# Six of eight query, key, value and gate preparations from scaled fp16 halves in three products, with the instruction order laid out anew

## The reference

```python
x = x + 0.5 * ffn(layernorm(x), W_gate, W_qkv)
x = x + attn(layernorm(x), gamma, beta, W_in, ...)
x = x + 0.5 * ffn(layernorm(x), W_gate, W_qkv)

def ffn(x, W_gate, W_qkv):                       # 16 heads of 16
    gating = softmax(x @ W_gate.T)               # one expert of 16 for each row
    indicator = one_hot(argmax(gating))
    q, k, v = split(x @ W_qkv.T, 3)
    k_shared = sum_h indicator[h] * k[h]         # one key and one value head for all queries
    v_shared = sum_h indicator[h] * top1 * v[h]
    att = softmax(causal(q_h @ k_shared.T / 4))
    return att @ v_shared
def attn(x, ...):                                # h = (1-a) h + a b, y = h * tanh(c)
    gates = layernorm2(x) @ W_in + b_in
    return scan(gates) @ W_out + x @ W_skip + biases
```

## Time and profile before

| | |
|---|---|
| median of three runs | 1006.3 us (1001.84 to 1007.03) |
| the profiled execution | 999.46 us |
| its span, first to last instruction | 997.6 us |
| PE busy | 920.5 us (92%) |
| DVE busy | 789.8 us (79%) |
| ACT busy | 702.9 us (70%) |
| POOL busy | 195.4 us (20%) |
| mean granted TensorE clock | 0.946 of full speed |

### The profile page before, as it was taken

The page is one execution under the profiler, slowest core; times in us unless marked ns, Lnnn a source line. Parts: engine busy times, 40 slices in busy tenths (PEclk is TensorE's granted clock), DMA queues, the critical chain, the costliest instruction groups (busy, mean ns, idle before and its releaser), DMA issues.

```text
span 997.6 us, 17809 instructions
## 1 busy us (share of the span) xinstructions
PE 920.5 (92%) x6071; PEld 308.5 (31%) x6071; DVE 789.8 (79%) x2257; ACT 702.9 (70%) x1136; POOL 195.4 (20%) x408
## 2 busy tenths in 40 slices
PE   8988798989899998999998999999999999999997
PEld 6433242223232332222332234332233222222222
DVE  4899689999869898896136999799897999899501
ACT  2255447867557858789868756767767887788896
POOL 2023302110222010012312312422101100101115
PEclk7799599979989999999999999999999998999999
DMA  5110010000100010000001000100001000000001
GB/s 158 54 54 2 1 48 8 1 2 2 54 1 1 2 54 2 1 1 2 1 19 36 1 1 12 44 1 23 1 10 46 1 2 22 2 1 2 3 1 43
DMA packets 20232, 17.94 MB, mean 18 GB/s; under 512 B 4128, under 2 KB 20144, under 8 KB 20144
## 3 DMA queue, kind: packets, MB, share of 16 engines
q1 hardware_dynamic: 19328, 16.00, 5.2%
q10 hardware_dynamic: 816, 0.80, 0.2%
HBM read 10.24 MB, written 6.29 MB: 17 GB/s over the span
## 4 chain that ended last, share of the span: by engine, by line
PE 47%; DVE 34%; ACT 8%; issue 7%; POOL 2%; DMA 1%; SPq 0%; POOLq 0%; DVEq 0%; ACTq 0%
PE ps L1514 16%; DVE ps L1253 15%; DVE mxp L1250 10%; PE ps L1480 9%; PE ps L1502 8%; ACT probs L1082 6%; PE ps L1413 4%; DVE mxp L1253 3%; PE ps L1418 2%; PE ps L1446 2%; DVE kv L1221 2%; PE ps L1408 1%; PE ps L1453 1%; ACT relu L1070 1%; DVE prod L1212 1%
## 5 line engine op out<-in xcount | busy, mean ns | idle before, releaser
L1082 ACT ACTIVATE probs<-ps 128x1024 f32<-128x1024 f32 (+5 forms) x794 | 550.1, 768 | 147.0 <-PE ps L1502 143.8
L1250 DVE TENSOR_REDUCE mxp<-ps 128x1 f32<-128x512 f32 x512 | 319.4, 682 | 31.2 <-PE ps L1480 29.9
L1514 PE MATMUL ps<-probs,v_l 128*32 128x512 f32 (+3 forms) x2560 | 309.1, 563 | 13.2 <-POOL probs L882 10.2
L1480 PE MATMUL ps<-k_tl,q_t 48*128 48x512 f16 (+3 forms) x1152 | 250.8, 360 | 12.5 <-DVE mxp L1253 5.9
L1502 PE MATMUL ps<-q_t,k_tl 50*128 50x512 f16 (+3 forms) x1280 | 231.3, 361 | 26.2 <-DVE mxp L1253 6.1
L1253 DVE CUSTOM_DVE_ANT_0 ps<-ps,mask 128x384 f32<-128x384 f32 (+3 forms) x512 | 232.9, 526 | 23.7 <-PE ps L1480 22.7
L882 POOL TENSOR_SCALAR_AFFINE_SELECT probs<-probs 128x256 f32<-128x256 f32 x256 | 103.0, 412 | 577.8 <-ACT probs L1082 574.7
L1480 PEld LDWEIGHTS ps<-k_tl,q_t 48*128 48x128 f16 x1152 | 72.7, 96 | 198.8 <-DVE mxp L1250 67.2
L1502 PEld LDWEIGHTS ps<-q_t,k_tl 50*128 50x128 f16 x1280 | 62.0, 94 | 208.5 <-ACT probs L1082 86.6
L1253 DVE DVE_READ_ACCUMULATOR2_ANT mxp<- 128x1 f32 x640 | 89.6, 140 | 0.0
L1514 PEld LDWEIGHTS ps<-probs,v_l 128*32 128x32 f32 x2560 | 54.7, 110 | 109.4 <-issue 79.8
(11 more groups left out here) (129 smaller groups left out, 555.4 us busy)
## 6 DMA issues: line engine op xcount, KB each, us to landing
q_t<-q_scratch SPq DMA_DIRECT2D x96, 64.0 KB, 2.1
q_scratch<-q_part SPq DMA_DIRECT2D x16, 256.0 KB, 2.1
x_sb<-in_L_attn_x_dram SPq DMA_DIRECT2D x4, 512.0 KB, 8.1
out_dram<-x_sb SPq DMA_DIRECT2D x4, 512.0 KB, 2.9
q_t<-m_row SPq DMA_DIRECT2D x64, 4.0 KB
wqkv_n<-in_L_ffn_W_qkv_dram ACTq DMA_DIRECT2D x1, 768.0 KB, 6.5
w_in_sb<-in_L_attn_W_in_dram SPq DMA_DIRECT2D x1, 384.0 KB, 5.7
w_skip_sb<-in_L_attn_W_skip_dram SPq DMA_DIRECT2D x1, 256.0 KB, 5.0
```

The costliest lines, as they stand in the source:

```text
L1082: last = a_.activation(out if len(banks) == 1 else out[:, n:n + 1, :], bank[:, :, P * i:QW], ACT.Exp, scale=SCALE / LIFT ** 2)
L1250: last = v_.tensor_reduce(to, scores, axis=AX, op=ALU.max)
L1480: last = mm(bank[:, col:col + w], q_rows(ROWS_X, c, g, hh, i * P, P), keys, start=True, stop=True)
L1514: last = mm(out_bank[VW * hh:VW * hh + VW, P * i:QW], v_l[:, l, kt, :], probs[:, s % NB, hh, P * i:QW], start=j == 0, stop=j == key_tiles( ...
```

## The change

All preparations but (0, 0) and (0, 1) take another way, which `fine(l, c)` names. The deviation is scaled so that `u` comes out 1024 times larger. A new entry `halve` on POOL writes `u` as an fp16 number and the fp16 rest, `u_x`. `turn` transposes both parts with an fp16 identity, and ACT copies twice as many fp16 columns out of the bank into `ut_x`. The weights are scaled by a power taken from their largest square and also split in two fp16 parts, `wqkv_x` and `wg_x`, once: entries `size`, `scale` (two) and `split` (three), on DVE, PE, POOL and ACT. A float32 matmul becomes three fp16 matmuls (large by large, large by small, small by large). The scales are taken out again where the results are read (`z_inv`, `z_w`).

The planner gets the new entries and other estimates (a masked maximum 115 instead of 75, q 2100 instead of 1800 where float32, the start of its clock windows), and `SIDE_WORK` other places. Attention, maxima and recurrence are computed as before.

```diff
-SIDE_WORK = [(-19, -4, prepare(0, 1)), (18, 18, [("bias",)]), (18, 25, prepare(0, 2)), (57, 57, prepare(0, 3)),
-             (57, 69, branch(0)), (81, 81, prepare(1, 0)), (118, 140, branch(1)), (141, 141, prepare(1, 1)),
-             (154, 174, branch(2)), (174, 175, prepare(1, 2)), (175, 196, branch(3)), (210, 216, prepare(1, 3))]
+SPLIT = [("scale", n) for n in range(2)] + [("split", n) for n in range(3)]
+SIDE_WORK = [(-31, -4, prepare(0, 1)), (-4, 6, [("size",)] + SPLIT), (18, 18, [("bias",)]),
+             (24, 24, prepare(0, 2)), (60, 60, prepare(0, 3)), (64, 64, branch(0)), (80, 84, prepare(1, 0)),
+             (118, 140, branch(1)), (140, 140, prepare(1, 1)), (147, 174, branch(2)), (174, 175, prepare(1, 2)),
+             (175, 196, branch(3)), (210, 215, prepare(1, 3))]
...
-        self.stretch, self.streamed, self.full = 0.0, 0.0, True
+        self.stretch, self.streamed, self.full = FIRST_W - 1.0, 0.0, True
...
+            def halve(e):
+
+                pool.wait_ge(s_ln, NO["norm", e[1], e[2]] + 1)
+                own(g_.tensor_copy(u_x[:, 0, :, :], u[:, :, :]))
+                g_.tensor_tensor(u_x[:, 1, :, :], u[:, :, :], u_x[:, 0, :, :], op=ALU.subtract).then_inc(s_half, 1)
...
+                g_.tensor_tensor(z_root[:, :], z_sq[:, :], z_exp[:, :], op=ALU.pow).then_inc(s_zroot, 1)
...
+                elif e[0] == "turn" and fine(e[1], e[2]):
+                    a_.activation(ut_x[:, e[3], :, :].rearrange("p a t -> p (a t)"), bank[:, :].bitcast(f16), ACT.Copy)\
+                        .then_inc(s_ra, 1)
...
+                a_.activation(to, of, ACT.Copy, scale=z_mul[:, 0:1]).then_inc(s_wh, 1)
...
+                for dc in range(DC):
+                    v_.tensor_tensor(squared[:, dc * 3 * D:dc * 3 * D + 3 * D], wqkv_t[:, dc, :], wqkv_t[:, dc, :], op=ALU.mult)
+                own(v_.tensor_tensor(squared[:, 6 * D:6 * D + DC * H].rearrange("p (a h) -> p a h", a=DC), wg_t[:, :, :],
+                                     wg_t[:, :, :], op=ALU.mult))
+                v_.tensor_reduce(z_part[:, 0:1], squared[:, 0:6 * D + DC * H], axis=AX, op=ALU.max).then_inc(s_size, 1)
...
+                    v_.tensor_copy(z_sq[:, :], bank[:, 0:1]).then_inc(s_rd, 1)
+                    dve.wait_ge(s_zroot, 1)
+                    own(v_.tensor_scalar(z_mul[:, :], z_root[:, :], W_SIZE, None, ALU.mult))
+                    own(v_.reciprocal(z_inv[:, :], z_mul[:, :]))
...
+                v_.scalar_tensor_tensor(to, of, z_mul[:, 0:1], first, ALU.mult, ALU.subtract).then_inc(s_wx, 1)
...
+                    for a in range(2):
+                        for t in range(TC):
+                            last = tr(parts[:, a * QW + t * P:a * QW + (t + 1) * P], u_x[:, a, t, dc * P:(dc + 1) * P],
+                                      ident_h[:, :])
...
+                products = [(0, 0), (0, 1), (1, 0)]
...
+                elif kind == "kv" and fine(l, c):
+                    t = e[3]
+                    for n, (dc, (a, b)) in enumerate((dc, ab) for dc in range(DC) for ab in products):
+                        last = mm(bank[:, :], ut_x[:, dc, a, t * P:(t + 1) * P], wqkv_x[:, b, dc, D:3 * D],
+                                  start=n == 0, stop=n == 3 * DC - 1)
```

More of the change, by code:

```diff
@@ L117, in prepare @@
 def prepare(l, c):
-    return [("stats", l, c), ("norm", l, c), ("turn", l, c, 0), ("turn", l, c, 1), ("gate", l, c), ("pick", l, c),
+    return [("stats", l, c), ("norm", l, c)] + ([] if (l, c) in SINGLE else [("halve", l, c)]) + [("turn", l, c, 0), ("turn", l, c, 1), ("gate", l, c), ("pick", l, c),
             ("q", l, c, 0), ("kv", l, c, 0), ("choose", l, c, 0), ("qout", l, c, 0), ("q", l, c, 1),
@@ L161 @@
     "oev": (0, [("ACT", 480)]), "fin": (460, [("DVE", 700), ("POOL", 750)]), "out": (0, []),
+    "size": (0, [("DVE", 3600)]), "halve": (0, [("POOL", 3600)]),
     "join": (0, [("DVE", 750)]), "row": (100, [("ACT", 230)]),
 }
+HALVED = {"turn": (560, [("ACT", 920)]), "gate": (1500, WEIGHT["gate"][1]), "kv": (1350, WEIGHT["kv"][1]),
+          "q": (1350, WEIGHT["q"][1])}
 TO_READER, TO_PE, TO_NEXT = 205, 240, 130
@@ L187, in weights @@
         return 1.75 * width(e[1]), "columns", []
+    if e[0] == "scale":
+        return 100, "full", [("DVE", 2300 if e[1] else 700)]
+    if e[0] == "split":
+        return 0, "full", [("ACT", 750), ("DVE", 900)]
+    if e[0] in HALVED and len(e) > 2 and e[1] < 2 and e[1:3] not in SINGLE:
+        return HALVED[e[0]][0], "full", HALVED[e[0]][1]
     if e[0] == "range":
@@ L191, in weights @@
         kind, _, pieces = BANKS[UNITS[e[1]][1]][e[2]]
-        return 226, "rows", [("ACT", 480) if kind == "diff" else ("DVE", 600 if kind == "part" else sum(75 + 1.04 * w for *_, w, _ in pieces))]
+        return 226, "rows", [("ACT", 480) if kind == "diff" else ("DVE", 600 if kind == "part" else sum(115 + 1.04 * w for *_, w, _ in pieces))]
     if e[0] == "warm":
@@ L205, in needs @@
     k = e[0]
-    if k in ("norm", "turn", "gate", "pick", "q", "qout", "kv", "choose", "kpack", "keys"):
+    if k in ("norm", "halve", "turn", "gate", "pick", "q", "qout", "kv", "choose", "kpack", "keys"):
         l, c = e[1:3]
-        return {"norm": [("stats", l, c)], "turn": [("norm", l, c)], "pick": [("gate", l, c)],
+        fine = l < 2 and (l, c) not in SINGLE
+        return {"norm": [("stats", l, c)], "halve": [("norm", l, c)], "turn": [("halve" if fine else "norm", l, c)], "pick": [("gate", l, c)],
                 "qout": [("q",) + e[1:]], "choose": [("kv",) + e[1:], ("pick", l, c)],
-                "kpack": [("choose", l, c, TC - 1)], "keys": [("kpack", l, c)]}.get(k, [("turn", l, c, 1)])
+                "kpack": [("choose", l, c, TC - 1)], "keys": [("kpack", l, c)]}.get(k, [("turn", l, c, 1)] + ([("split", 2)] if fine else []))
     if k in ("dpack", "dkeys"):
@@ L218, in needs @@
         return [("rec", e[1], 1), ("skip", e[1], 1)]
+    if k in ("scale", "split"):
+        return [("scale", 1)] if k == "split" else [("scale", 0)] if e[1] else [("size",)]
     return [("squares",) if e[1] == 0 else ("range", 0)] if k == "range" else []
@@ L548, with fine @@
         _last = _e
+HALVES = [_e for _e in ORDER if _e[0] == "halve"]
+def fine(l, c):
+    return l < 2 and (l, c) not in SINGLE
 TURNS = [_e for _e in ORDER if _e[0] == "turn" and _e[3] == DC - 1]
@@ L1317, in _ @@
                     stats_of(e)
+                elif e[0] == "size":
+                    size()
+                elif e[0] == "scale":
+                    scales(e)
+                elif e[0] == "split":
+                    split(e)
                 elif e[0] == "squares":
```

116 lines of the change are left out of this document (104 added, 12 removed).

## The result

The changed kernel took 969.24 us (median of four, 966.6 to 972.44), the kernel before 1004.07 us beside it (four, 997.36 to 1007.03): ratio 0.966, 95% interval 0.9615 to 0.9706. The profiled execution, 972.44 us, is the slowest of the four. Single runs of the kernel before lie between 997 and 1010 us in all sessions, so a ratio of medians of a few runs is good to about 5 us.

What follows compares the result with a forecast made beforehand. PE and DVE were taken to share the bound, with PE setting the pace in the six changed preparations. -15.8 + 6 + 1 + 1 - 3 - 2 = -12.8 us off 1006.3 gave 993.5 us, range 983 to 1007.

Steps and rivals of the forecast that it cites:

- The order: Masks ahead of the statistics behind the bias entry, -3 us (bounds 0 and -5); warm matmuls at the head, -2 us.
- Products: On PE in six preparations: six fp16 matmuls replace two float32 ones, 0.52 us saved for each of 36, 18.7 us.
- three quarters: Share of PE's 21 us saved on products and gate that was counted as reaching the end: -15.8 us.
- Gate: On PE in six preparations: 24 fp16 matmuls in 1.4 us instead of 1.80, 2.4 us saved.
- Scales and split: Once, at about 75 to 100 us: 8.2 us on DVE, partly coming back later, taken as +6 us.
- Halve: On POOL between norm and turn: 3.4 us in each of six preparations, covered by spacing in the order, +1 us.
- ACT: Twice as many columns copied in each preparation, 4.9 us, mostly hidden; with the split's copies +1 us.
- (a): Rival: all of PE's 21 us arrive and the head keeps its clock, about 985 us; chance 0.15.
- (b): Rival: DVE is the bound, the split costs 8.2 us, a quarter of the products arrives, 1006 to 1008 us; chance 0.14.
- (c): Rival: PE's clock falls more often, in three more preparations, +6, about 1000 us; chance 0.07.
- (e): Rival: the products' fp16 matmuls each wait for weights and run at record length, about 1025 us; chance 0.02.
- (d): Rival: masks wait behind halve on POOL, PE stands and loses clock in four preparations, about 1018 us; chance 0.06.

Runs made afterwards that it cites:

- f1: Changed kernel's own list, frozen, without the halve, size, scale and split entries, everything in float32: 984.75 us, 0.9848 of the kernel before.
- a4: Changed kernel with the planner's clock windows started from 0 as before: 993.96 us, 0.9928 of the kernel before.
- b1: Changed kernel in its own order with two more fp16 matmuls ahead of each of the 36 products: 983.08 us, 0.9787 of the kernel before.
- b4: Changed kernel in its own order with cast and subtraction done twice in each halve: 993.2 us, 0.9878 of the kernel before.
- g1: Frozen list of the kernel before with the fp16 parts put in by hand, nothing else moved: 1017.82 us, 1.0178 of the kernel before.
- a3: Changed kernel with the old estimate of 75 for a masked maximum: 1027.37 us, 1.0251 of the kernel before.

## Why the prediction was wrong

**Direction right, and the mechanism of the parts; the sum 21 us short.** Of the 34 us, f1 gives 15.2 to the order and leaves 18.8 (give or take 5) to the parts. By the two profiled spans it is 14.6 and 12.3, and the plain medians of f1 and the changed kernel are 15.5 us apart; the profiled execution of the changed kernel was its slowest, so the ratios weigh more.

**The order: -3 and -2 forecast, -15 measured.** This is the first step that failed. I judged a new list of a whole program from two places. Both places came out as said: behind the bias entry no mask wait over 0.3 us is left (3.32 in the earlier trace rows), and the head is 2.4 us ahead, though a4 shows that the warm matmuls need not be the reason. But neither is where most of the order's effect lies. The bounds 0 and -5 should have come from how much a list can be worth at all. The runs show that: in float32, lists that differ by one number range from 0.9726 to 1.0142. The row that could have warned me was the sum over the whole span, 77.1 us of PE idle time and 48.3 of excess at 1.2 GHz, which any list redistributes.

**Products: -18.7, three quarters counted.** The duration was right. The share was near as far as the runs can tell: b1 says 0.8 with a wide interval, the whole table 0.6, its three late steps 0.6 to 1.05.

**Gate: -2.4 forecast, -7.2 on PE.** Mis-sized, because I took 0.053 us a matmul from transposes of 128 columns, and 16 columns cost 0.025. The prediction set a figure of the Trainium skill, "TensorE: Matmul & The Clock Gate", section Back-to-back issue gap, against this term, and misread it: the 81 ns a pair hold for 128 streamed columns, and the gate streams 16. The same section's table for matmuls without loads has about 60 cycles, the floor of some 25 ns, for up to 64 columns, and the trace agrees, 0.025 us, with a load for each. At 128 columns the trace is below the 81 ns: the 16 transposes of the turn, with a load each, took 1.00 us from start to start, 0.063 each. The prediction also took the whole 3.2 us off its sum where its own three quarters would have made it 2.4.

**Scales and split: +6 forecast, +3 measured** at the same list. What is seen of it is the delay of one `y_att`. **Halve: +1.** The price of 3.2 us was right, and its cover holds in the list that was planned with it: of its mechanism one wait of 2.22 us and some smaller ones are seen. b4 and g1 show what it costs without cover: 22 us (give or take 7) for a second one, and 15 us of waits. **ACT: +1.** Its busy time is 5.6 us more, as worked out (4.9 and the split's copies); no run isolates its effect.

With the gate at -7.2, products and gate at 0.8 and +3 for the scales, the parts sum to -20.7 + 3 + 1 + 1 = -15.7, inside the measured 19 give or take 5. With -15 for the order that would have been -31.

**The rivals.** (a), all PE time arrives, was closest in number (985), but for another reason: it had no more for the order than the forecast's bounds, and neither b1 nor the table can tell its full share from three quarters. (b), DVE as the bound, is out: the gain arrives in steps at the preparations. (c) and (e) are out: mean clock 0.951, products 1.3 us apart. (d) happened once. It would have been the result had the entries gone into the old list: g1 stands at 1017.8, and I had given 1018 for (d). That match is luck: what stands there is first the turns and the maxima behind `size`, and not the masks (9.0 us in g1, 10.2 before).

**Open.** Why one list beats another is shown only as its sums, clock and idle, not as a cause that could be told ahead. g1 is one placement by hand; another in the old list may lose less. And the split of the 34 us depends on the way: parts first is +18 and then -52, order first is -15 and then -19. The best list in float32 that was run gave 0.9726, so against it the parts with their own list are 0.7% ahead, just outside what the two intervals leave open (0.62%).

## What to carry to other kernels

Where a planner draws the order, freeze its list before pricing a change: run the new list with the old work, and the old list with the new work. A single estimate moved this kernel by up to 6% (0.966 to 1.025) with the same arithmetic, and 115 and 116 alone differ by 1.35%, so a run that changes one number of a planner may show a draw, not that number's worth; take several neighbouring values before believing in one. A new instruction between two others that are planned close can cost most of its length at each place until the plan knows of it (here 2.5 of 3.2 us, at six of six).

## What was not expected of the hardware

24 fp16 matmuls with 16 columns each, every one with a load of 128 columns of weights, took 0.60 us from start to start: 0.025 us a pair of load and matmul. And two kernels with the same instructions but for ten warm matmuls spent about 96 us (after) and 181 us (a3) at the lower clock, by stretches of 4 us: the order of the same work moved it.
